# Local softmax sums: the last 64 keys joined in by an add on GpSimd, two matmul groups in place of four, and a new hand-written time table

## The reference

```python
rel = k_idx - W - q_idx                       # W = 64
win = (rel >= -pad) & (rel <= pad - 1)        # pad = 32: a band of 64 keys for each query
attn_local = softmax(where(win & in_range, q k^T * scale, NEG))
out_local = attn_local @ v
attn_g = softmax(q @ k[::W]^T * scale)        # 128 global keys
out_global = attn_g @ v[::W]
out = (out_local + out_global) @ w_out + b_out
```

## Time and profile before

| | |
|---|---|
| median of 3 runs | 3414.16 us (3412.81 to 3414.69) |
| time of the profiled execution | 3419.38 us |
| its span, first to last instruction | 3417.6 us |
| TensorE busy | 3338.3 us, 98% |
| VectorE, ScalarE, GpSimd busy | 73%, 58%, 56% |
| granted TensorE clock, mean | 0.987 |

### The profile page before, as it was taken

The page is one execution under the profiler, slowest core; times in us unless marked ns, Lnnn a source line. Parts: engine busy times, 40 slices in busy tenths (PEclk is TensorE's granted clock), DMA queues, the critical chain, the costliest instruction groups (busy, mean ns, idle before and its releaser), DMA issues.

```text
span 3417.6 us, 72834 instructions
## 1 busy us (share of the span) xinstructions
PE 3338.3 (98%) x24916; PEld 2508.1 (73%) x24916; DVE 2491.0 (73%) x4425; ACT 1993.9 (58%) x3876; POOL 1915.6 (56%) x2961
## 2 busy tenths in 40 slices
PE   8999999999999699999999999999999999999997
PEld 6888888888888467777777777777777777777775
DVE  4444544445444578988898888988898889888986
ACT  2222322222222567777777777777777777777772
POOL 0000000000000378888788878888888878887885
PEclk9999999999999689999999999999999999999999
DMA  7778778787788656766667666776676666766651
GB/s 186 234 207 242 220 215 239 209 239 223 207 240 239 140 107 142 161 148 142 142 146 160 138 138 144 165 159 139 142 161 148 142 142 149 159 140 137 144 133 38
DMA packets 538325, 572.77 MB, mean 168 GB/s; under 512 B 55752, under 2 KB 354344, under 8 KB 538024
## 3 DMA queue, kind: packets, MB, share of 16 engines
q1 hardware_dynamic: 457992, 533.97, 62.6%
q10 hardware_dynamic: 79744, 34.70, 5.7%
q0 software_dynamic: 288, 0.20, 0.1%
HBM read 330.98 MB, written 203.23 MB: 156 GB/s over the span
## 4 chain that ended last, share of the span: by engine, by line
PE 58%; DVE 5%; POOL 2%; issue 1%; ACT 1%; ACTq 0%; POOLq 0%; DVEq 0%
PE ps_misc L1215 18%; PE ps_mx L1111 9%; PE ps_sc L1133 7%; PE ps_os L1167 5%; PE ps_os L1186 5%; PE ps_os L1192 4%; PE ps_sc L1152 3%; PE ps_os L1199 3%; PE ps_sc L1224 2%; DVE qk L1007 1%; PE ps_os L1170 1%; DVE bnb L989 1%; DVE r_loc L1033 1%; PE ps_sc L1121 1%; DVE r_glob L1033 1%
## 5 line engine op out<-in xcount | busy, mean ns | idle before, releaser
L1007 DVE TENSOR_REDUCE qk<-ps_mx 128x10 f32<-128x640 f32 x1024 | 809.4, 805 | 130.3 <-PE ps_mx L1111 119.1
L962 ACT ACTIVATE ps_mx<-mask 128x640 f32<-128x640 bf16 x1022 | 715.1, 706 | 124.3 <-DVE qk L1007 113.1
L520 PE MATMUL po<-ht_hi,w_both 128*128 128x512 f32 x2048 | 639.0, 391 | 1.5 <-ACT ht_hi L302 1.5
L933 ACT ACTIVATE qk<-ps_sc 128x384 f32<-128x384 f32 (+1 forms) x1024 | 443.4, 459 | 298.0 <-PE ps_sc L1133 242.6
L520 PEld LDWEIGHTS po<-ht_hi,w_both 128*128 128x128 f32 x2048 | 385.3, 188 | 86.3 <-issue 4.1
L883 POOL TENSOR_SCALAR_AFFINE_SELECT qk<-qk 128x512 f32<-128x512 f32 (+1 forms) x512 | 317.6, 620 | 233.1 <-ACT qk L933 228.0
L520 PE MATMUL po<-ht_lo,w_both 128*128 128x512 f32 x1024 | 399.2, 390 | 0.0
L886 POOL TENSOR_SCALAR_AFFINE_SELECT qk<-qk 128x512 f32<-128x512 f32 x512 | 335.3, 655 | 35.0
L524 PE MATMUL po<-w_both,ht_hi 128*128 128x512 f32 x1024 | 320.6, 389 | 1.3 <-DVE w_both L371 1.3
L946 ACT ACTIVATE v<-ps_sc 128x512 f32<-128x512 f32 x512 | 297.0, 593 | 33.3 <-PE ps_sc L1152 33.3
L893 POOL TENSOR_TENSOR qk<-qk 128x256 f32<-128x256 f32 x384 | 290.8, 767 | 10.7
(11 more groups left out here) (159 smaller groups left out, 7843.0 us busy)
## 6 DMA issues: line engine op xcount, KB each, us to landing
xb<-in_L_attn_x SPq DMA_DIRECT2D x256, 256.0 KB, 6.3
w_both<-q_hi_d SPq DMA_DIRECT2D x256, 256.0 KB
q_lo_d<-o_lo SPq DMA_DIRECT2D x32, 1024.0 KB, 8.6
k_lo_d<-o_lo SPq DMA_DIRECT2D x32, 1024.0 KB, 10.1
w_both<-q_lo_d SPq DMA_DIRECT2D x128, 256.0 KB
vw<-v_d SPq DMA_DIRECT2D x128, 256.0 KB, 5.0
out<-xb SPq DMA_DIRECT2D x128, 256.0 KB, 3.2
bt<-at ACTq DMA_DIRECT2D x496, 64.0 KB, 6.0
```

What stands on the lines that cost most here:

```text
L520: last = nc.tensor.matmul(po[bank(o, u)][:], wa[:, k, o * P:(o + 1) * P], ha[u][:, k, :], start=start, stop=stop)
L933: nc.scalar.activation(p_loc[:, tile, 2 * hp:2 * hp + 2, lo:MW], ps_sc[n % 2][:, 0:2 * MW].rearrange("p (h n) -> p h n", h=2)[:, :, lo:MW] ...
L962: nc.scalar.activation(ps_mx[u % 2][:, :, 0:MWG], mask[:, turn:turn + 1, :].to_broadcast([P, 2, MWG]), ACT.Copy).then_inc(seeded, 1)
L1007: nc.vector.tensor_reduce(mb[s % 2][:, heads, tile, :], ps_mx[u % 2][:, :, 0:MWG].rearrange("p h (b n) -> p h b n", n=WIN), axis=AX.X, op= ...
```

## The change

GpSimd gets a fourth `sadd` in each step, which adds the masked exponentials of the last 64 keys to the second half of the last tile. `p_last` gets 128 partitions for it, of which the upper 64 are set to zero once, at the start of the stage, by a memset on GpSimd that follows its two others and has its own wait. `p_sum` grows from three to four parts, so the small tiles that lay behind it move to tiles of their own. `sl` has two groups of 256 columns in place of the four, and waits for `s_added` at `4 * s + 4` alone; the fourth `sadd` waits for the last `locm` and for `lastm`. `sl` and `sg` stay separate items. All three tables of times are new.

```diff
-        p_sum = qk_rest[:, 0:12 * WIN].bitcast(F32).rearrange("p (i h n) -> p i h n", i=3, h=4)
+        p_sum = qk_rest[:, 0:16 * WIN].bitcast(F32).rearrange("p (i h n) -> p i h n", i=4, h=4)
...
-        p_last = sb("p_last", [WIN, 4, WIN], F32)
+        p_last = sb("p_last", [P, 4, WIN], F32)
...
-        small = qk_rest[:, 12 * WIN:12 * WIN + 2 * (blocks + joined)].bitcast(F32)
+        small = sb("small", [P, 2 * (blocks + joined)], F32)[:]
...
-        PERIOD = 16.5
+        PERIOD = 16.2
         STEP = {
...
-            "loc": (0.847, 1.259, 1.445, 5.277, 1.584, 4.812, 10.1, 10.414),
-            "x_loc": (5.038, 3.297, 1.239, 4.532, 1.974, 9.777, 3.433, 8.956),
-            "locm": (4.363, 2.995, 7.078, 11.037),
-            "sadd": (4.613, 13.682, 11.307),
+            "loc": (1.383, 2.375, 1.842, 4.975, 2.282, 3.933, 10.968, 11.199),
+            "x_loc": (2.117, 5.597, -0.515, 3.825, 2.763, 9.145, 6.526, 14.745),
+            "locm": (5.356, 5.381, 8.742, 12.531),
+            "sadd": (13.062, 9.548, 6.994, 13.534),
...
-            "glob": (6.183, 11.975, 7.166, 13.419),
+            "glob": (5.891, 14.465, 6.909, 14.158),
...
-            "ol": (14.033, 13.563, 14.113),
-            "oc": (16.127,),
-            "sl": (17.694,),
-            "sg": (17.911,),
+            "ol": (15.672, 16.407, 15.739),
+            "oc": (14.656,),
+            "sl": (17.611,),
+            "sg": (18.382,),
...
-            "olm": (21.594,),
-            "osum": (25.997,),
+            "olm": (25.69,),
+            "osum": (27.527,),
...
-            "otl": (53.185, 27.844, 37.238, 32.356),
+            "otl": (45.079, 35.121, 35.574, 31.722),
...
                 for g in range(EARLY, GROUPS):
                     stacks.set_keys(pool, g)
+                for g in range(EARLY, GROUPS):
+                    pool.wait_ge(stacks.k_made[g], 1)
+                pool.memset(p_last[WIN:P], 0.0).then_inc(rest_zeroed, 1)
+                pool.wait_ge(rest_zeroed, 1)
...
                     if name == "sadd":
-                        pool.wait_ge(loc_masked, 4 * s + i + 2)
-                        pool.tensor_tensor(p_sum[:, i, :, :], p_loc[:, i, :, P:MW], p_loc[:, i + 1, :, 0:WIN], ALU.add).then_inc(s_added, 1)
+                        if i < 3:
+                            pool.wait_ge(loc_masked, 4 * s + i + 2)
+                            pool.tensor_tensor(p_sum[:, i, :, :], p_loc[:, i, :, P:MW], p_loc[:, i + 1, :, 0:WIN], ALU.add).then_inc(s_added, 1)
+                        else:
+                            pool.wait_ge(loc_masked, 4 * s + 4)
+                            pool.wait_ge(last_masked, s + 1)
+                            pool.tensor_tensor(p_sum[:, i, :, :], p_loc[:, i, :, P:MW], p_last[:], ALU.add).then_inc(s_added, 1)
...
                     if name == "sl":
                         pe.wait_ge(o_copied, s + 1)
-                        pe.wait_ge(s_added, 3 * s + 3)
-                        pe.wait_ge(loc_masked, 4 * s + 4)
-                        pe.wait_ge(last_masked, s + 1)
+                        pe.wait_ge(s_added, 4 * s + 4)
                         halves = ps_os[:].rearrange("p (t b n) -> p t b n", b=2, n=WIN)
-                        for n, (sums, windows) in enumerate(((halves[:, 0:3, 0, :], p_loc[:, 0:3, :, WIN:P]),
-                                                             (halves[:, 0:3, 1, :], p_sum[:]),
-                                                             (ps_os[:, CHUNK - P:CHUNK], p_loc[:, 3, :, WIN:MW]),
-                                                             (ps_os[:, CHUNK - WIN:CHUNK], p_last[:]))):
+                        for n, windows in enumerate((p_loc[:, :, :, WIN:P], p_sum[:])):
                             for h in range(4):
-                                window = windows[:, :, h, :] if len(windows.shape) == 4 else windows[:, h, :]
-                                last = nc.tensor.matmul(sums[h * DH:(h + 1) * DH], ones[0:windows.shape[0], 0, :], window,
+                                last = nc.tensor.matmul(halves[h * DH:(h + 1) * DH, :, n, :], ones[:, 0, :], windows[:, :, h, :],
                                                         start=n == 0, stop=False, skip_group_check=True)
```

More of the change, by code:

```diff
@@ L690, in attention_phase @@
         mv = [sb(f"mvb{s}", [P, TILES, 2], F32) for s in range(3)]
-        ve = [sb(f"veb{s}", [P, TILES], F32) for s in range(3)]
-        rs = [sb(f"rsb{s}", [P, TILES], F32) for s in range(3)]
-        nm = sb("nmb", [P, TILES], F32)
+        ln_small = sb("ln_small", [P, 7, TILES], F32)
+        ve, rs, nm = [ln_small[:, s, :] for s in range(3)], [ln_small[:, 3 + s, :] for s in range(3)], ln_small[:, 6, :]
         ps_mx = [pb(f"ps_mx{b}", [P, 2, 512]) for b in range(2)]
@@ new lines, in attention_phase @@
+            "max": (-22.887, -22.834, -15.469, -14.829, -12.951, -17.502, -13.02, -10.835),
+            "maxr": (-21.654, -20.459, -15.069, -13.127, -19.668, -11.572, -10.812, -11.939),
+            "seed": (-25.445, -20.05, -16.881, -18.137, -13.825, -7.886, -11.813, -2.505),
+            "maxc": (-10.438,),
+            "mt": (-6.696,),
+            "x_mt": (-5.76,),
+            "loc": (1.383, 2.375, 1.842, 4.975, 2.282, 3.933, 10.968, 11.199),
+            "x_loc": (2.117, 5.597, -0.515, 3.825, 2.763, 9.145, 6.526, 14.745),
@@ new lines, in attention_phase @@
+            "locm": (5.356, 5.381, 8.742, 12.531),
+            "sadd": (13.062, 9.548, 6.994, 13.534),
+            "last": (4.267,),
+            "x_last": (2.491,),
+            "lastm": (8.58,),
+            "glob": (5.891, 14.465, 6.909, 14.158),
+            "x_glob": (13.382, 7.474, 8.895, 11.641),
+            "ol": (15.672, 16.407, 15.739),
+            "oc": (14.656,),
+            "sl": (17.611,),
+            "sg": (18.382,),
+            "sums": (20.132,),
+            "pvgo": (20.538,),
@@ L776, in attention_phase @@
[L776 to L780 removed]
+            "out": (22.709, 25.612, 18.77, 23.5, 31.627, 28.459, 30.304, 30.378, 38.439, 34.854, 42.451, 39.825, 45.834, 45.75, 39.032, 42.967),
@@ new lines, in attention_phase @@
+            "outa": (24.948, 31.866, 38.655, 44.361),
+            "outs": (25.323, 33.442, 42.943, 47.294),
+            "rs0": (32.819, 26.317, 49.892, 44.716),
+            "x1": (30.149, 36.161, 44.632, 51.702),
+            "x1s": (34.2, 37.014, 46.773, 51.905),
+            "rs1": (40.183, 33.059, 53.21, 51.242),
+            "x1n": (35.892, 41.33, 52.011, 57.809),
+            "tr": (41.113, 49.447, 57.547, 66.121),
+            "x_tr": (41.442, 46.932, 56.081, 61.229),
+            "trl": (42.371, 51.395, 57.809, 67.094),
@@ L781, in attention_phase @@
+            "ffn": (51.522, 49.75, 55.304, 55.691, 61.366, 62.245, 58.879, 58.385, 67.335, 73.062, 74.068, 70.225, 77.5, 76.61, 80.237, 76.96),
+            "ffna": (54.764, 64.492, 72.196, 78.816),
+            "ffns": (75.379, 65.823, 79.682, 59.147),
+            "rs2": (63.855, 84.389, 86.009, 62.665),
+            "za": (76.866, 78.541, 92.711, 82.482),
         }
@@ L1169, in item @@
                                 else:
-                                    last = nc.tensor.matmul(ps_os[rows, CHUNK - WIN:CHUNK], vl[s % V_BUFS][:, head], p_last[:, h, :],
+                                    last = nc.tensor.matmul(ps_os[rows, CHUNK - WIN:CHUNK], vl[s % V_BUFS][:, head], p_last[0:WIN, h, :],
                                                             start=False, stop=True, skip_group_check=True)
```

39 lines of the change are left out of this document (7 added, 32 removed).

## The result

| | before | after |
|---|---|---|
| median | 3415.77 us (20 runs) | 3422.28 us (20 runs) |
| least | 3410.3 us | 3418.66 us |
| span of the profiled execution | 3417.6 us | 3419.4 us |

After / before is 1.0021, with a 95% interval of 1.0014 to 1.0028: some 7 us slower. One of the 20 runs after took 3550.84 us at a granted clock of 0.90 and is left out of the ratio. The forecast was 3372 us in a range of 3350 to 3402.

A forecast was written before the change was run, and what follows sets the result against it. TensorE's chain of waits was taken to bound the kernel: 32 us from the local sums plus 10 from the last mask, 42 in all, off a median of 3414.2 gave 3372 us, in a range of 3350 to 3402.

The forecast's parts named there:

- TensorE sets the time, one for one: Second stage: what leaves TensorE's queue shortens the 69.28 us chunk one for one, until another engine's work comes last.
- The local sums, 32 us: `sl` on TensorE: two groups for four take 1.00 us instead of 1.25, saving 0.25 us in each of 128 steps.
- only the columns: Rival on the local sums: only the removed 64 columns come back, 14 us, giving 3400 us; chance 0.14.
- the 19 us: Local sums priced by columns and a floor of some 2.5 ns per matmul: 0.15 us a step.
- The fourth add at no cost: GpSimd's extra 128x256 addition a step is hidden by its idle time; without cover it would cost 90 us.
- The fit "by 0.17 to 0.2 us": Behind the last mask, GpSimd's adds finish before TensorE reaches `sl`: 1.38 against 1.55 us, or 2.63 against 2.84.
- GpSimd comes too late: Rival: adds behind the last mask delay `sl`; slower, 3470 us with the whole add on the path; chance 0.11.
- The last mask, 10 us: `ol` waiting at tile 3's mask: the new order removes half of 0.16 us a step (20 us in all).
- The rest of the order: Stalls the new order might bring in other loops: not priced, only widening the forecast's tails.
- VectorE takes up what TensorE gives: Rival: VectorE, 88% busy and 90% after, swallows the gain; no change, 3408 to 3420 us; chance 0.07.
- absorbed: Each new add stretching a VectorE residual add by 0.2 us costs 6 us, against 61 us idle in 532.
- the loop "`max`, `maxr`, `seed`": VectorE would need some 1 us a chunk more on this loop to swallow the gain.

The follow-up runs named there:

- run 6: Kernel before with only VectorE's join of the maxima rewritten as two reductions with one input each: 3406.33 us, ratio 0.9968.
- run 9: Kernel before (four groups, three adds) with the new tables of times and the single-input join: 3386.36 us, ratio 0.9910.
- run 5: Kernel after with VectorE's two-input join replaced by two reductions with one input each, order and sums unchanged: 3355.27 us, ratio 0.9819.
- runs 10: Kernel after with the old tables of times, fourth add directly behind the third, and the single-input join: 3430.26 us, ratio 1.0034.
- run 7: Kernel after with one `rs0` time moved back, so that root stands behind `osum` in one step of four: 3408.75 us, ratio 0.9973.
- run 4: Kernel before with the new tables of times, old sums and no fourth add: 3436.61 us, ratio 1.0069.
- run 2: Kernel after with GpSimd's `olm` multiplication cut into two instructions of 256 columns in the same place: 3392.28 us, ratio 0.9937.
- run 1: Kernel after with `olm` moved ahead of `lastm` and the third `locm` again, one table time altered: 3394.5 us, ratio 0.9943.
- run 12: Kernel after with single-input join, `rs0` behind `osum`, and `olm` moved ahead of `lastm`: 3349.18 us, ratio 0.9798.

## Why the prediction was wrong

The runs with the single-input join split the change into parts. Each is a difference of ratios, in per cent of before, with 1% = 34.2 us:

| step | ratio | worth |
|---|---|---|
| before | 1.0000 | |
| its two-input join taken away (run 6) | 0.9968 | -11 us |
| new order (run 9) | 0.9910 | -20 us |
| new sums with the fourth add (run 5) | 0.9819 | -31 us |
| two-input join back: the kernel after | 1.0021 | +69 us |

**TensorE sets the time, one for one**. Right for before and for run 5, and the reasoning with chunks holds in both, but the pieces were not all TensorE's: once a chunk, from 2035.50 to 2039.75, the chain of before already runs through VectorE, and the join is its last piece there. The "DVE 5%" of the earlier trace rows stands for that. It failed for after, since other engines' work entered the chain, as the text allowed for but didn't find.

**The local sums, 32 us.** Right: 31 us, 1.00 us of chain a step, a chunk shorter by 1.00 us. The rival "only the columns" (14 us) is refuted by run 9 against run 5. So are the 19 us that I estimated from the Trainium skill's page "TensorE: Matmul & The Clock Gate", section "Back-to-back issue gap". I had used its formula outside its scope: the page calls the formula one for an isolated matmul and says that it counts too little for few columns, so the page isn't what the measurement contradicts.

**The fourth add at no cost.** Right in the new order: run 5 has the whole gain, and `sl` waited for line 902 for 1.2 us in all. The fit "by 0.17 to 0.2 us" was enough. In the old order the rival "GpSimd comes too late" is what happens: with one add more behind the last mask it turns a gain of 31 us into a loss of 23 (runs 10 and 6). Its place was told rightly; the new order avoids it.

**The last mask, 10 us.** Nothing came of it on balance. From the first matmul of line 1167 to the first of line 1170, the four steps of a chunk took 1.53, 1.50, 1.47 and 1.45 us in the median; the forecast took all to be near 1.50. After, three take 1.33, which is 11 us over the run, and the fourth takes 1.90 instead of 1.50, which loses 10: the sum is 194.1 us before and 193.0 after. I didn't look at what GpSimd waits for in front of that mask: of its items I counted durations, and not the idle time that a moved item such as `rs0` brings with it, nor what VectorE does beside them.

**The rest of the order.** The new order without holds of the join is worth 20 us. I gave it 10, all for the last mask. So the 20 come from parts that were unpriced, and that they came out on the good side is luck; which parts they are wasn't found.

**The step that failed** is the price of contention in the rival "VectorE takes up what TensorE gives". I saw that something stretches VectorE's instructions by up to 1 us, named GpSimd as a candidate, and then priced it as 0.2 us for each new add on the residual adds `x1` and `za`, which nobody waits for soon: "absorbed". Three things are wrong in that. The residual adds don't get longer: their medians go from 911 and 748 ns to 743 and 745, and what gets longer is the join. The price isn't a share of the add, but what remains of whichever GpSimd instruction is under way, up to the 1.29 us of `olm`, and in 27 steps the next one as well. And the instruction to ask about is the one that TensorE waits for, `maxc`, then `mt`. Its row in before (184/295/842 ns) showed that something lengthens it; I named the loop "`max`, `maxr`, `seed`" and the roughly 1 us a chunk it would need, but read neither that row nor where the new table puts `olm` against `maxc`. The wait in that row, 12.3 us in 32 steps, wouldn't have given the price: 30 of the 32 follow a join of 0.19 us that nothing held, like this one of before, on the path and beside the small instruction of line 911:

```profile
2039.36 0.30 POOL L911 TENSOR_SCALAR nmb<-mvb,rsb 128x1 f32<-128x1 f32 x1
2039.42 0.19 DVE L1020 TENSOR_TENSOR qk<-qk 128x16 f32<-128x16 f32 x1
...
2039.75 0.27 PE L1121 MATMUL ps_sc<-ident,qk 128*32 128x128 f32 x1 [0.32 <-DVE qk L1020]
```

The old order had its holds mostly where TensorE didn't wait; the new one put them where it does. The two-input join costs 69 us in the new order and 11 in the old; the net cost of 58 us eats the 51 us that order and sums bring. The 69 us are not all TensorE's wait for line 1029 (55.5 us); the held join also delays VectorE's later items, as in run 7. How the remainder splits wasn't measured.

That the hold is the cause is shown four ways: the order alone brings it (run 4), a shorter GpSimd instruction shortens it (run 2), moving it relieves it in part (run 1), and instructions of nearly the same work with one input don't suffer it (run 5). That the rewritten join is also a little quicker by itself is no rival: in the old order all of the edit gives 11 us (run 6).

## What to carry to other kernels

Before a new order of work is priced, list VectorE's instructions with two SBUF inputs on which another engine waits, however small, and ask which GpSimd instruction is under way when each starts: price the hold at the rest of that instruction, and of the next if it follows at once. Ask the same of GpSimd's instructions on the path, and of what VectorE does beside them. A spread such as 184/295/842 ns on a 16-column instruction is the sign to look for. Where it is on the path, rewriting the small instruction with one SBUF input cost nothing here, and the place of `olm` then mattered no more (run 12). An instruction with one of its inputs in PSUM (line 1048) wasn't held either; moving the join's input there wasn't tried.

## What the hardware showed unexpectedly

- A maximum over 128x16 elements takes 0.186 us at least and 1.23 to 1.32 us when it meets a 1.29 us multiplication on GpSimd; it ends 0.04 us behind it in both places looked at. Beside two selects, of 0.41 and 0.63 us, it takes 0.85 to 0.98. Reductions with one input beside it stay at 141 to 186 ns (line 1026, all 128), and line 1048, with one input in PSUM, at 672 to 691 ns (all 128), even at 2047.34 in run 5, begun 0.03 us behind an `olm`.
- It goes the other way too: a select on GpSimd takes 1.09 us instead of 0.64 beside a residual add on VectorE with two inputs in SBUF, an add 1.16 instead of 0.73.
- A small group costs more than its columns: 8 matmul instructions of 64 columns and 64 keys cost 0.25 us, where their columns alone were put at 0.11, while 24 of 192, 192 and 128 columns, 16 of 256 and 8 of 512 take 1.00 us each. Whether the few columns or the 64 keys make the difference isn't separated here.
